# Rotary embedding of the second attention: order, number and memory of the VectorE instructions between the two attentions

## The chip, the cores and the metric

The kernel runs on one core of one Trainium2 chip. The metric is the device time of one execution in microseconds (us); the median of three runs is taken. TensorE does the matrix products, ScalarE (ACT in the profile) activations and copies, VectorE (DVE) and GpSimd (POOL) elementwise work; SyncE (SP) issues DMAs. PSUM is the memory into which TensorE writes, SBUF the large on-chip memory. GpSimd works on SBUF alone here.

## The reference

Two transformer layers over 2048 tokens of width 128, all in float32. Layer 0: a layer norm, an attention of 16 heads of 8 with an arccos kernel instead of softmax, and a gated feed-forward part, both added to the input. Layer 1, cut to what matters:

```
xn  = layernorm(x);  xa = layernorm(xn) * gamma + beta
q, k, v = split(xa @ w_qkv)                 # 16 heads of 64, each of q, k, v: 2048 x 1024
rotate(t): t1, t2 = halves of a head (32 + 32)
           [t1*cos - t2*sin, t2*cos + t1*sin]
scores = rotate(q) rotate(k)^T / 8;  out = softmax(scores) v;  x + out @ w_out + b_out + ffn(xn)
```

The change concerns `rotate` for q and k: 2048 tokens by 2048 values (q and k together).

## The kernel before

The program is a sequence of blocks: `stage_project0`, `stage_attention0`, `stage_project1`, `stage_attention1`, `stage_output`. Between blocks all engines meet. The change is in `stage_project1`, the stage between the attentions. It adds the output of attention 0 to the residual, does two layer norms and then a loop over 16 tiles (`k`) of 128 tokens each. The times and rows below speak mostly of this loop.

For each tile TensorE makes six banks of 512 float32 columns (`qkv(k, b)`, L1084, two matmuls per bank): b = 0 to 3 are q and k and go to the four banks of `psR`, b = 4 and 5 are v and go to the two banks of `psA`. A unit u = 4k + b is one bank of `psR`, which is 8 heads of q or k. A unit passes through these steps, each on its own engine, tied by semaphores:

1. VectorE rotates: cosine product from PSUM to `ra` (L965), two sine products of half the size from PSUM to `rb` (L967, L969), and the sum `ra + rb` into `ra` (L973). `ra` and `rb` have two buffers each (u % 2).
2. ScalarE rounds `ra` to float16 into `hl` (`high_qk`, L1004).
3. GpSimd computes the rest `ra - hl` into `hl` (L1048, semaphore `lo_ready`).
4. TensorE transposes the eight heads into `psB` (`turn_halves`, L1093).
5. ScalarE copies `psB` to `stg` (`stage`, L1023), and after every fourth tile (at the end after every second) SyncE stores `stg` to HBM.

For v, ScalarE writes a rounded half (`high_v`, L1013) and VectorE the rest (L979), two instructions per tile behind the four units. TensorE may overwrite bank b of `psR` with the next tile when the semaphore `rope_read` says so: before, that is at the end of the second sine product. `ra` is written again when `lo_ready` of unit u - 2 has come. The order of work on each engine is the order in which it is written in the code; there is no planner. On TensorE this order is: qkv(k+1,0), qkv(k+1,1), turn_halves(k,0), qkv(k+1,2), turn_halves(k,1), qkv(k+1,3), turn_halves(k,2), qkv(k+1,4), qkv(k+1,5), turn_halves(k,3). On ScalarE, per tile: high_qk 0, stage 3 of the tile before, high_v 0, high_qk 1, high_v 1, high_qk 2, stage 0, high_qk 3, stage 1, stage 2.

Of the kernel before, what the change touches and what calls it, by code (L numbers as in the profile page):

```python
# [6 lines left out]
ALU = mybir.AluOpType  # L7
# [7 lines left out]
P = 128  # L15
S = 2048
D = 128
NT = S // P
# [827 lines left out]
def stage_project1(nc, io, sb):  # L846
# [3 lines left out]
    HB = 8  # L850
    HALF = HD1 // 2
    with ExitStack() as ctx:
        def t(name, shape, dt=F32):
            return ctx.enter_context(nc.sbuf_tensor(name, shape, dt))

        def sem(name):
            return ctx.enter_context(nc.semaphore(name))
# [8 lines left out]
        cos_t, sin_t = t("cos_t", [P, NT, HALF]), t("sin_t", [P, NT, 2, HALF])  # L866
        ident_h = t("ident_h", [P, P], F16)
        ra, rb = t("ra", [P, 2, BANK]), t("rb", [P, 2, BANK])
# [4 lines left out]
        psR = ctx.enter_context(nc.psum_tensor("psR1", [P, 4, BANK], F32))  # L873
# [7 lines left out]
        xn_ready, xa_ready = sem("xn_ready1"), sem("xa_ready1")  # L881
        qkv_ps, rope_read = sem("qkv_ps1"), sem("rope_read")
        v_high, v_low = sem("v_high"), sem("v_low")
        rot_ready, hi_ready, lo_ready = sem("rot_ready"), sem("hi_ready"), sem("lo_ready")
        hl_ps, hl_taken = sem("hl_ps"), sem("hl_taken")

        v_stored = [sem("v_stored_0"), sem("v_stored_1")]
# [3 lines left out]
        with nc.Block() as block:  # L891
# [32 lines left out]
            @block.vector  # L924
            def _(eng):
                n = [0]

                def link(ins):
                    n[0] += 1
                    ins.then_inc(dve, 1)  # L930
                    eng.wait_ge(dve, n[0])

                eng.wait_ge(weights_loaded, 16 * 6)
                eng.tensor_copy(ident_h[:, :], ident[:, :])
                eng.memset(v_st[:, :, :, :, HD1:HD1 + 1], QS)
                eng.memset(v_st[:, :, :, :, VN:VW], 0.0)
                link(eng.tensor_tensor(base[:, :, :], base[:, :, :],
                                       b_out[:, :].unsqueeze(1).to_broadcast([P, NT, D]), ALU.add))
                for k in range(NT):
                    eng.wait_ge(out_ps, k + 1)  # L940
                    eng.tensor_tensor(base[:, k, :], base[:, k, :], psR[:, k % 4, 0:D], ALU.add).then_inc(x1_ready, 1)
                eng.wait_ge(x1_ready, NT)
                norm_on_vector(eng, link, base, xn, stats, mv, var, sd, tmp, var_ready, sd_ready, 1)
                eng.sem_inc(xn_ready, 1)
                norm_on_vector(eng, link, xn, xa, stats, mv, var, sd, tmp, var_ready, sd_ready, 2)
                link(eng.tensor_tensor(xa[:, :, :], xa[:, :, :], gamma[:, :].unsqueeze(1).to_broadcast([P, NT, D]),
                                       ALU.mult))
                eng.tensor_tensor(xa[:, :, :], xa[:, :, :], beta[:, :].unsqueeze(1).to_broadcast([P, NT, D]),
                                  ALU.add).then_inc(xa_ready, 1)

                eng.tensor_tensor(base[:, :, :], base[:, :, :], b_out1[:, :].unsqueeze(1).to_broadcast([P, NT, D]),
                                  ALU.add)

                eng.wait_ge(loaded, 32)
                for k in range(NT):
                    for b in range(4):
                        u = 4 * k + b

                        src = psR[:, b, :].rearrange("p (h a f) -> p h a f", h=HB, a=2)
                        a_ = ra[:, u % 2, :].rearrange("p (h a f) -> p h a f", h=HB, a=2)  # L960
                        b_ = rb[:, u % 2, :].rearrange("p (h a f) -> p h a f", h=HB, a=2)
                        eng.wait_ge(qkv_ps, 6 * k + b + 1)
                        if u >= 2:
                            eng.wait_ge(lo_ready, u - 1)
                        eng.tensor_tensor(a_, src, cos_t[:, k, :].unsqueeze(1).unsqueeze(1)  # L965
                                          .to_broadcast([P, HB, 2, HALF]), ALU.mult)
                        eng.tensor_tensor(b_[:, :, 0, :], src[:, :, 1, :],  # L967
                                          sin_t[:, k, 0, :].unsqueeze(1).to_broadcast([P, HB, HALF]), ALU.mult)
                        eng.tensor_tensor(b_[:, :, 1, :], src[:, :, 0, :],  # L969
                                          sin_t[:, k, 1, :].unsqueeze(1).to_broadcast([P, HB, HALF]), ALU.mult)\  # L970
                           .then_inc(rope_read, 1)
                        eng.wait_ge(rope_read, u + 1)
                        eng.tensor_tensor(ra[:, u % 2, :], ra[:, u % 2, :], rb[:, u % 2, :], ALU.add)\  # L973
                           .then_inc(rot_ready, 1)
                    for b in range(2):

                        eng.wait_ge(v_high, 2 * k + b + 1)
                        vv = v_st[:, k // 4 % 2, b * HB:(b + 1) * HB, k % 4, :]
                        eng.scalar_tensor_tensor(out=vv[:, :, HD1 + 1:VN],  # L979
                                                 in0=psA[:, b, :].rearrange("p (h e) -> p h e", h=HB), scalar=QS,  # L980
                                                 in1=vv[:, :, 0:HD1], op0=ALU.mult, op1=ALU.subtract)\
                           .then_inc(v_low, 1)

            @block.scalar
            def _(eng):
                for g in range(NCH):
                    eng.wait_ge(turned, g + 1)
                    eng.activation(attn0T[:, g * BANK:(g + 1) * BANK], psA[:, g % 2, :], ACT.Copy).then_inc(taken, 1)
                for i in range(2):
                    eng.wait_ge(var_ready, i + 1)  # L990
                    eng.activation(sd[:, :], var[:, :], ACT.Sqrt).then_inc(sd_ready, 1)
                    for g in range(NCH):
                        eng.wait_ge(turned, NCH * (i + 1) + g + 1)
                        dst = (xn2T, xaT)[i]
                        eng.activation(dst[:, g * BANK:(g + 1) * BANK], psA[:, g % 2, :], ACT.Copy).then_inc(taken, 1)

                def high_qk(k, b):

                    u = 4 * k + b
                    eng.wait_ge(rot_ready, u + 1)  # L1000
                    if k >= 2:

                        eng.wait_ge(hl_ps, 4 * (k - 1))
                    eng.activation(hl[:, k % 2, b * HB:(b + 1) * HB, 0, :],  # L1004
                                   ra[:, u % 2, :].rearrange("p (h e) -> p h e", h=HB), ACT.Copy)\
                       .then_inc(hi_ready, 1)

                def high_v(k, b):
                    eng.wait_ge(qkv_ps, 6 * k + 5 + b)
                    if k == 8 or k == 12:  # L1010

                        eng.wait_ge(v_stored[k // 4 % 2], 16)
                    eng.activation(v_st[:, k // 4 % 2, b * HB:(b + 1) * HB, k % 4, 0:HD1],  # L1013
                                   psA[:, b, :].rearrange("p (h e) -> p h e", h=HB), ACT.Copy, scale=QS)\
                       .then_inc(v_high, 1)

                def stage(k, g):

                    eng.wait_ge(hl_ps, 4 * k + g + 1)
                    if k % 4 == 0 and k >= 8:  # L1020

                        eng.wait_ge(qk_stored[k // 4 % 2], 32 * (k // 8))
                    eng.activation(stg[:, k // 4 % 2, g * HB:(g + 1) * HB, k % 4 * P:(k % 4 + 1) * P],  # L1023
                                   psB[:, g % 2, :].rearrange("p (h t) -> p h t", h=HB), ACT.Copy)\
                       .then_inc(hl_taken, 1)

                for k in range(NT):
                    high_qk(k, 0)
                    if k >= 1:
                        stage(k - 1, 3)  # L1030
                    high_v(k, 0)
                    high_qk(k, 1)
                    high_v(k, 1)
                    high_qk(k, 2)
                    stage(k, 0)
                    high_qk(k, 3)
                    stage(k, 1)
                    stage(k, 2)
                stage(NT - 1, 3)
# [620 lines left out]
```

## Time and profile before

| | |
|---|---|
| median of 3 runs | 3676.81 us (3673.8 to 3677.45) |
| the profiled execution: time, span | 3673.4 us, 3671.6 us |
| granted TensorE clock, mean over the span | 0.831 |
| loop over the 16 tiles, first VectorE instruction to last ScalarE instruction | 1996.40 to 2167.58 us |
| share of the span: PE, DVE, ACT, POOL | 85%, 77%, 82%, 73% |

A time in the profile is in microseconds from the start of the span. "DVE L973 ... 1.15" is the duration of one instruction; a bracket at the end of a line tells how long the engine stood idle before it and what it waited for. An instruction can start a little before the end that is shown for the one in front of it on its engine, so the spacing of two starts can be less than a duration.

### The profile page before, as it was taken

The page shows a single profiled execution, that of the slowest core. Times are in us where ns is not written, and L with a number is a line of the kernel's source. Part 1 is how long each engine was busy: PE and PEld are TensorE (multiplying, and loading weights), DVE is VectorE, ACT ScalarE, POOL GpSimd, SP SyncE. Part 2 cuts the span into 40 slices and gives each one's busy share as a digit, 9 for nine tenths or more (in the row PEclk, how much of TensorE's full clock was granted, in tenths as well). Part 3 has the DMA queues.
Part 4 walks back from the last instruction along what each step waited for, and adds up shares of the span by engine and source line. Part 5 has one row for each costly group of instructions (what it writes and reads, how often), then busy time and mean ns, then how long its engine had stood idle before and what let it go on. Part 6 is the DMA issues. An engine that isn't in the chain of part 4 may idle for free. (4 is left out here: it accounts for less than half of the span.)

```text
span 3671.6 us, 59781 instructions
## 1 busy us (share of the span) xinstructions
PE 3125.7 (85%) x19264; PEld 1305.2 (36%) x19264; DVE 2831.9 (77%) x4045; ACT 3014.8 (82%) x2658; POOL 2666.5 (73%) x1450
## 2 busy tenths in 40 slices
PE   4888888898888988889886758888888888888899
PEld 2322222222122221222213323555555555555547
DVE  7678988888888888888887977877878778788301
ACT  1799999999999999999995645887878888788822
POOL 2698988989889898898882424776767777677600
PEclk8776677766777667776677977999999999999999
DMA  0100000000000000000001450010000110000100
GB/s 23 53 7 7 1 6 7 6 7 2 4 7 6 7 4 3 7 6 6 5 5 38 139 161 24 25 47 25 24 25 24 34 38 24 25 24 25 39 0 12
DMA packets 59508, 85.46 MB, mean 23 GB/s; under 512 B 9808, under 2 KB 45904, under 8 KB 58960
## 3 DMA queue, kind: packets, MB, share of 16 engines
q1 hardware_dynamic: 59344, 83.06, 7.9%
q8 instruction: 129, 2.11, 0.2%
q14 instruction: 35, 0.29, 0.0%
HBM read 52.44 MB, written 30.54 MB: 23 GB/s over the span
## 5 line engine op out<-in xcount | busy, mean ns | idle before, releaser
L1177 POOL TENSOR_TENSOR lo<-pr,hi 128x1024 f16<-128x1024 f32 x384 | 917.3, 2412 | 383.8 <-ACT hi L1303 381.7
L1226 DVE TENSOR_REDUCE mx<-mx_ps 128x1 f32<-128x512 f32 x1024 | 660.0, 684 | 164.8 <-PE mx_ps L1341 161.5
L1318 ACT ACTIVATE pr<-s_ps 128x1024 f32<-128x1024 f32 x512 | 531.8, 1039 | 264.3 <-PE s_ps L1362 234.7
L1303 ACT ACTIVATE hi<-pr 128x1024 f16<-128x1024 f32 x512 | 548.1, 1071 | 0.0
L1341 PE MATMUL mx_ps<-ka,qa 128*128 128x512 f16 x1024 | 386.1, 398 | 142.4 <-DVE mx L1226 117.3
L671 ACT ACTIVATE wt<-wt 128x2048 f32<-128x2048 f32 x256 | 485.0, 1895 | 0.5
L477 POOL TENSOR_TENSOR wt<-base,wt 128x1024 f32<-128x1024 f32 x192 | 459.9, 2395 | 15.1
L662 ACT ACTIVATE wt<-wt,theta_bias 128x10240 f32<-128x10240 f32 (+2 forms) x96 | 464.3, 4837 | 0.8
L1381 PE MATMUL pv_ps<-vh,hi 128*128 128x129 f16 x4096 | 432.0, 222 | 11.6 <-ACT sums L1309 5.3
L1360 PE MATMUL s_ps<-qa,ka 128*128 128x512 f16 x1024 | 395.9, 387 | 35.2 <-issue 22.4
L473 POOL TENSOR_TENSOR base<-base,shift 128x1024 f32<-128x1024 f32 x192 | 363.7, 1894 | 84.6 <-DVE base L527 84.6
L1381 PE MATMUL pv_ps<-vh,lo 128*128 128x65 f16 x4096 | 417.9, 194 | 0.0
L1362 PE MATMUL s_ps<-qb,kb 65*128 65x512 f16 x1024 | 396.6, 387 | 0.0
L1381 PEld LDWEIGHTS pv_ps<-vh,hi 128*128 128x128 f16 x4096 | 372.1, 98 | 61.8 <-POOL lo L1177 11.5
L477 POOL TENSOR_TENSOR wt<-vb,wt 128x1024 f32<-128x1024 f32 x160 | 379.0, 2369 | 12.6
L1381 PEld LDWEIGHTS pv_ps<-vh,lo 128*128 128x128 f16 x4096 | 365.9, 98 | 55.9 <-issue 3.0
L750 PE MATMUL m_ps<-mst 110*128 110x512 f16 (+1 forms) x640 | 321.2, 609 | 47.5 <-ACT wt L651 19.7
L643 ACT ACTIVATE wt<-m_ps 128x1024 f32<-128x1024 f32 x352 | 333.1, 1033 | 25.8 <-PE m_ps L719 24.2
L473 POOL TENSOR_TENSOR vb<-vb,shift 128x1024 f32<-128x1024 f32 x160 | 302.9, 1893 | 60.3 <-DVE vb L527 60.3
L750 PE MATMUL r_ps<-mst 111*128 111x512 f16 (+1 forms) x768 | 315.0, 446 | 35.2 <-DVE wt L515 10.3
L1177 DVE TENSOR_TENSOR lo<-pr,hi 128x1024 f16<-128x1024 f32 x128 | 261.8, 2046 | 86.6 <-ACT hi L1303 86.6
L719 PE MATMUL m_ps<-mst 109*128 109x512 f16 x1024 | 308.3, 385 | 22.0 <-ACT wt L643 11.2
(197 smaller groups left out, 5292.7 us busy)
## 6 DMA issues: line engine op xcount, KB each, us to landing
qk<-stg SPq DMA_DIRECT2D x6, 2048.0 KB, 13.4
vh<-v SPq DMA_DIRECT2D x16, 520.0 KB, 3.5
qa<-qk SPq DMA_DIRECT2D x16, 512.0 KB, 3.3
ka<-qk SPq DMA_DIRECT2D x32, 256.0 KB, 4.8
v<-v_st SPq DMA_DIRECT2D x3, 2080.0 KB, 7.9
qst<-parts_dram SPq DMA_DIRECT2D x144, 32.0 KB
kst<-parts_dram SPq DMA_DIRECT2D x144, 32.0 KB
qk<-stg SPq DMA_DIRECT2D x4, 1024.0 KB, 8.7
```

Source lines behind the costliest of these rows:

```text
L473: eng.tensor_tensor(v, v, shift[:, 0:1].to_broadcast([P, 2 * BANK]), ALU.subtract)\
L477: eng.tensor_tensor(u, v, u, ALU.mult).then_inc(cubic, 1)
L662: eng.activation(wt[:, k:k + many, :], wt[:, k:k + many, :], ACT.Ln, bias=theta_bias[:, 0:1], scale=-2.0 if k >= NQ else -KA / (G4 * G4 * ...
L671: eng.activation(wt[:, k, :], wt[:, k, :], ACT.Exp, scale=GEXP, accum_out=n_c[:, k:k + 1])\
L750: mm = eng.matmul(slot(r)[:, cols(i, BANK)], mst[0:rows, 1, cols(k)], mst[0:rows, 0, rhs], start=True, stop=True)
L1177: eng.tensor_tensor(lo[:, i % NHL, :, :], pr_slot(i), hi[:, i % NHL, :, :], ALU.subtract).then_inc(lo_done, 1)
L1226: eng.tensor_reduce(mx4[:, q // NCH, q % NCH:q % NCH + 1], mx_ps[:, q % 2, :], AX.X, ALU.max)\
L1303: eng.activation(hi[:, i % NHL, :, :], pr_slot(i), ACT.Copy).then_inc(hi_done, 1)
L1318: eng.activation(pr_slot(i), s_ps[:, i % 2, :, :], ACT.Exp, scale=SM).then_inc(exp_done, 1)
L1360: eng.matmul(s_ps[:, i % 2, n_, :], ka[:, par, k * P:(k + 1) * P], qa[:, par, w], start=True, stop=False)
L1362: mm = eng.matmul(s_ps[:, i % 2, n_, :], kb[0:HD1 + 1, par, k * P:(k + 1) * P], qb[0:HD1 + 1, par, w], start=False, stop=True)
L1381: mm = eng.matmul(pv_ps[:, j // 2, j % 2 * OW:j % 2 * OW + cols], half[:, i % NHL, n_, j * P:(j + 1) * P], vh[:, par, k, 0:cols], start=(k ...
```

## The change

The sine product becomes one instruction of 512 elements per partition, which reads the bank with the halves of each head exchanged and writes `rb`. It comes first. The cosine product reads the same bank of `psR` and writes its result over it, in place. The sum then reads `psR` (PSUM) and `rb` (SBUF) and writes `ra`. `rope_read`, which allows TensorE to overwrite the bank, now comes with the sum, and ScalarE waits for the same semaphore in place of `rot_ready`. The instructions of neighbouring units are interleaved: sine(u), sum(u-1), cosine(u). For the last unit of all tiles but the last one, the sum comes after the two v instructions and the first sine product of the next tile.

```diff
+                def halves(ap):
+                    return ap.rearrange("p (h a f) -> p h a f", h=HB, a=2)
+                def sine(u):
+                    k, b = u // 4, u % 4
+                    eng.wait_ge(qkv_ps, 6 * k + b + 1)
+                    if u >= 2:
+                        eng.wait_ge(rope_read, u - 1)
+                    eng.tensor_tensor(halves(rb[:, u % 2, :]), halves(psR[:, b, :])[:, :, ::-1, :],
+                                      sin_t[:, k, :, :].unsqueeze(1).to_broadcast([P, HB, 2, HALF]),
+                                      ALU.mult).then_inc(sin_ready, 1)
+                def cosine(u):
+                    k, b = u // 4, u % 4
+                    eng.wait_ge(sin_ready, u + 1)
+                    eng.tensor_tensor(halves(psR[:, b, :]), halves(psR[:, b, :]),
+                                      cos_t[:, k, :].unsqueeze(1).unsqueeze(1).to_broadcast([P, HB, 2, HALF]),
+                                      ALU.mult).then_inc(cos_ready, 1)
+                def rotated(u):
+                    eng.wait_ge(cos_ready, u + 1)
+                    if u >= 2:
+                        eng.wait_ge(lo_ready, u - 1)
+                    eng.tensor_tensor(ra[:, u % 2, :], psR[:, u % 4, :], rb[:, u % 2, :], ALU.add)\
+                       .then_inc(rope_read, 1)
                 for k in range(NT):
-                    for b in range(4):
-                        u = 4 * k + b
-                        src = psR[:, b, :].rearrange("p (h a f) -> p h a f", h=HB, a=2)
-                        a_ = ra[:, u % 2, :].rearrange("p (h a f) -> p h a f", h=HB, a=2)
-                        b_ = rb[:, u % 2, :].rearrange("p (h a f) -> p h a f", h=HB, a=2)
-                        eng.wait_ge(qkv_ps, 6 * k + b + 1)
-                        if u >= 2:
-                            eng.wait_ge(lo_ready, u - 1)
-                        eng.tensor_tensor(a_, src, cos_t[:, k, :].unsqueeze(1).unsqueeze(1)
-                                          .to_broadcast([P, HB, 2, HALF]), ALU.mult)
-                        eng.tensor_tensor(b_[:, :, 0, :], src[:, :, 1, :],
-                                          sin_t[:, k, 0, :].unsqueeze(1).to_broadcast([P, HB, HALF]), ALU.mult)
-                        eng.tensor_tensor(b_[:, :, 1, :], src[:, :, 0, :],
-                                          sin_t[:, k, 1, :].unsqueeze(1).to_broadcast([P, HB, HALF]), ALU.mult)\
-                           .then_inc(rope_read, 1)
-                        eng.wait_ge(rope_read, u + 1)
-                        eng.tensor_tensor(ra[:, u % 2, :], ra[:, u % 2, :], rb[:, u % 2, :], ALU.add)\
-                           .then_inc(rot_ready, 1)
+                    for u in range(4 * k, 4 * k + 4):
+                        sine(u)
+                        if u >= 1:
+                            rotated(u - 1)
+                        cosine(u)
+                    if k == NT - 1:
+                        rotated(4 * NT - 1)
...
                 def high_qk(k, b):
-                    eng.wait_ge(rot_ready, u + 1)
+                    eng.wait_ge(rope_read, u + 1)
```

## Rows read from the trace of the kernel before

**Rows 1.** The profile's page: the span, and VectorE's busy time over it.

```profile
span 3671.6 us, 59781 instructions
...
PE 3125.7 (85%) x19264; PEld 1305.2 (36%) x19264; DVE 2831.9 (77%) x4045; ACT 3014.8 (82%) x2658; POOL 2666.5 (73%) x1450
```

**Rows 2.** Busy time by stretch: the loop; granted clock (PEclk), DMA share behind it.

```profile
1995.00:2164.00 169.00, 128.53 (x696) 63.49 (x696) 165.39 (x287) 111.57 (x158) 72.74 (x63) 0.98 0.42 132
```

**Rows 3.** Waits in the loop, 1996 to 2180: total us, times, longest.

```profile
ACT hl L1004 <- DVE ra L973: 56.8, 64, 3.4
...
DVE ra L965 <- PE psR L1084: 3.6, 1, 3.6
```

**Rows 4.** Groups of instructions, VectorE, same stretch: busy us, mean ns.

```profile
L973 DVE TENSOR_TENSOR ra<-ra,rb 128x512 f32<-128x512 f32 x64 | 66.1, 1033 | 2.2
L965 DVE TENSOR_TENSOR ra<-psR,cos_t 128x512 f32<-128x512 f32 x64 | 43.4, 679 | 3.6 <-PE psR L1084 3.6
```

**Rows 5.** Timeline of VectorE over one tile: start us, duration us.

```profile
2058.32 1.28 DVE L979 SCALAR_TENSOR_TENSOR v_st<-psA,v_st 128x512 f16<-128x512 f32 x2
2059.52 0.68 DVE L965 TENSOR_TENSOR ra<-psR,cos_t 128x512 f32<-128x512 f32 x1
2060.12 0.41 DVE L967 TENSOR_TENSOR rb<-psR,sin_t 128x256 f32<-128x256 f32 x1
2060.45 0.41 DVE L969 TENSOR_TENSOR rb<-psR,sin_t 128x256 f32<-128x256 f32 x1
2060.89 0.69 DVE L973 TENSOR_TENSOR ra<-ra,rb 128x512 f32<-128x512 f32 x1
2061.50 0.68 DVE L965 TENSOR_TENSOR ra<-psR,cos_t 128x512 f32<-128x512 f32 x1
...
2062.43 0.41 DVE L969 TENSOR_TENSOR rb<-psR,sin_t 128x256 f32<-128x256 f32 x1
2062.88 1.15 DVE L973 TENSOR_TENSOR ra<-ra,rb 128x512 f32<-128x512 f32 x1
2063.95 0.68 DVE L965 TENSOR_TENSOR ra<-psR,cos_t 128x512 f32<-128x512 f32 x1
...
2068.84 1.28 DVE L979 SCALAR_TENSOR_TENSOR v_st<-psA,v_st 128x512 f16<-128x512 f32 x2
```

**Rows 6.** Timeline of GpSimd over the same tile.

```profile
2059.14 1.16 POOL L1048 TENSOR_TENSOR hl<-ra,hl 128x512 f16<-128x512 f32 x1 [1.29 <-ACT hl L1004]
2062.33 1.15 POOL L1048 TENSOR_TENSOR hl<-ra,hl 128x512 f16<-128x512 f32 x1 [2.03 <-ACT hl L1004]
```

**Rows 7.** The first VectorE instruction, the last sum and the last ScalarE copy.

```profile
1996.40 0.69 DVE L965 TENSOR_TENSOR ra<-psR,cos_t 128x512 f32<-128x512 f32 x1 [3.55 <-PE psR L1084]
...
2162.39 1.15 DVE L973 TENSOR_TENSOR ra<-ra,rb 128x512 f32<-128x512 f32 x1
...
2166.56 1.02 ACT L1023 ACTIVATE stg<-psB 128x1024 f16<-128x1024 f16 x1 [0.53 <-PE psB L1093]
```

**Rows 8.** Tile t_ps in attention 0: duration ns, minimum/median/maximum.

```profile
L582 DVE TENSOR_TENSOR t_ps<-t_ps,small x16: 184/185/190, 329.4 to 1955.7; 128x16 f32<-128x16 f32 x16
...
L588 DVE TENSOR_TENSOR small<-small,t_ps x16: 181/183/185, 330.1 to 1956.5; 128x16 f32<-128x16 f32 x16
```

**Rows 9.** Groups of instructions, ScalarE, in the loop.

```profile
L1023 ACT ACTIVATE stg<-psB 128x1024 f16<-128x1024 f16 x64 | 62.9, 1008 | 0.5 <-PE psB L1093 0.5
L1004 ACT ACTIVATE hl<-ra 128x512 f16<-128x512 f32 x64 | 40.3, 630 | 56.8 <-DVE ra L973 56.8
L1013 ACT ACTIVATE v_st<-psA 128x512 f16<-128x512 f32 x32 | 18.7, 584 | 0.6 <-PE psA L1084 0.6
```

**Rows 10.** Timeline of TensorE where it runs without waits, early in the loop.

```profile
2000.42 1.88 PE L1084 MATMUL psR<-w_qkv,attn0T 128*128 128x512 f32 x4
...
2002.14 0.61 PE L1093 MATMUL psB<-ident_h,hl 128*128 128x128 f16 x8
...
2002.58 1.08 PE L1084 MATMUL psR<-w_qkv,attn0T 128*128 128x512 f32 x2
```

More of the change, by code:

```diff
@@ L883, in stage_project1 @@
         v_high, v_low = sem("v_high"), sem("v_low")
-        rot_ready, hi_ready, lo_ready = sem("rot_ready"), sem("hi_ready"), sem("lo_ready")
+        sin_ready, cos_ready = sem("sin_ready"), sem("cos_ready")
+        hi_ready, lo_ready = sem("hi_ready"), sem("lo_ready")
         hl_ps, hl_taken = sem("hl_ps"), sem("hl_taken")
```

## The prediction

> **What bounds the kernel now.** I read the page first: no engine is busy all the time (DVE 77% of a span of 3671.6 us, [rows 1]), so the answer lies in the stage of the change. Its loop over 16 tiles, between about 1995 and 2168 us, is a different picture: in a stretch of 169.0 us VectorE is busy 165.4 us, TensorE 128.5, ScalarE 111.6, GpSimd 72.7, at a granted clock of 0.98 [rows 2]. The waits say the same from the other side. ScalarE waits 64 times, 56.8 us in all, for VectorE's sum, while VectorE has waited once, 3.6 us, before the first unit [rows 3]. VectorE bounds the loop, all of its instructions are in series, and what shortens them shortens the kernel: the engines meet behind the stage, and nothing of the next stage starts earlier by itself.
>
> The timeline of one tile shows what the time goes to [rows 5]. From the pair of v instructions at 2058.32 to the next pair at 2068.84 it is 10.52 us; 16 times 10.52 is 168.3, which is the loop. Spacing of starts: a product of 512 elements 0.60 (2059.52 to 2060.12), a sine half 0.33, the second half 0.44, because the sum behind it waits for its end (0.41 + 0.03), the sum 0.61 or 1.07. The sums are of two kinds, 0.69 and 1.15 us. The mean of 64 is 1033 ns [rows 4], which is 48 of 1.15 and 16 of 0.69: three of four are long. The long one at 2062.88 starts while GpSimd runs from 2062.33 to 2063.48, the short one at 2060.89 behind the end of a GpSimd run (2059.14 + 1.16 = 2060.30) [rows 5, 6]. So a sum of two SBUF operands is stretched by 0.46 us when GpSimd works beside it.
>
> Products with one operand in PSUM are not: the cosine product at 2059.52 lies wholly under the GpSimd run that ends at 2060.30 and takes 0.68, and the sine half at 2062.43 lies wholly under the next and takes 0.41, as those outside do [rows 5, 6].
>
> **The change, part by part.** It has four effects on VectorE, per tile:
>
> 1. The sum reads PSUM and SBUF, as the cosine product did. By the rows it should then cost that product's 0.68 us, spacing 0.60, GpSimd or not. Three sums fall from 1.07 to 0.60 and one from 0.61 to 0.60: 1.42 us.
> 2. Two sine halves become one instruction: 0.33 + 0.33 becomes 0.60, four times 0.06: 0.24 us. The exchanged halves are runs of 32 elements, which each half read before at no cost that shows: 0.409 against 0.679 us for 256 against 512 elements is 1.05 ns per element and a fixed part. Were the single instruction as dear as the halves, 0.24 us is lost again.
> 3. The wait of the sum for the instruction right in front of it goes: sine(u), sum(u-1), cosine(u) each wait for something at least two places back. Four times 0.11: 0.44 us.
> 4. The cosine product writes PSUM, the bank that it reads. This form at this size is not in the trace. The nearest rows are 16 elements wide: 185 ns in place in PSUM, 183 ns to SBUF [rows 8]. The 2 ns are 0.13 ns per element, or 0.06 us at 512 elements, 4 us in 64 units. A bank that served a read or a write by turns would double 1.05 ns per element; 16 elements would then show 17 ns, not 2. I take 0, with 4 us as the mild upper end; no row speaks for a gain.
>
> The new tile is 12 instructions at 0.60 and two v instructions at 0.60 (2058.32 to 2059.52 is 1.20 for two): 8.40 us. 10.52 - 8.40 = 2.12, and the parts give 1.42 + 0.24 + 0.44 = 2.10.
>
> From the first VectorE instruction to the end of the last sum it is now 2163.54 - 1996.40 = 167.1 us [rows 7]. In the new order 64 + 64 + 63 products and sums and 30 v instructions precede the last sum: 221 x 0.60 + 0.11 (it does wait for the cosine in front of it) + 0.68 = 133.4. The edge takes 1.0 back, see below: 134.4. The tail (rounding, rest, transposes, copy: 4.0 us to 2167.58) and the stores behind it stay. That is 32.7 us less. A second semaphore on an instruction may cost 0.01 (0.61 behind a sum, 0.60 behind a cosine [rows 5]); sine and sum both carry two, 127 x 0.01 = 1.3. I take 32.
>
> Two rules of the Trainium skill speak for less. "VectorE: DVE Perf Modes", section on the TRN2 errata, gives a PSUM source a fixed part of 120 cycles and an SBUF source 58; at 0.96 GHz that is 0.065 us more per sum, 4.1 us in all. The rows have 0.679 us for the product out of PSUM and 0.69 for the unstretched sum out of SBUF [rows 4, 5], no such step. The same page, section "The DRAIN you can't avoid", says that a semaphore between Vector instructions costs nothing; by it part 3 would be worth nothing, 7.0 us less. The rows have 0.33 us of spacing without and 0.44 with the wait behind the same shape [rows 5]. By both rules the gain would be about 21 us.
>
> **Can the others keep a pace of 8.40?** ScalarE has 4 x 1.008 + 4 x 0.630 + 2 x 0.584 = 7.72 us per tile [rows 9], less in spacing. TensorE, where it runs free, needs 1.72 us for two banks and 0.44 for eight transposes [rows 10]: 6 x 0.86 + 4 x 0.44 = 6.9. GpSimd 4 x 1.15 = 4.6. All fit, ScalarE with least room.
>
> Two loops get tighter. The bank of `psR` is freed at the sum: about 3.1 us after the start of its sine instead of 1.4 after the start of its cosine. The same bank's next sine starts at least 7.2 us after the last one, so 4 us are left for two matmuls of 1.1; TensorE has, in its queue, transposes ahead of them, but no wait longer than that chain. The two buffers of `ra` are tighter: sum(u) needs the rest of u-2. From the start of a sum: 0.68 + 0.03 + 0.63 (rounding) + 0.08 + 1.15 (rest) + 0.03 = 2.60 us, against 3.60 for two units. That leaves 1.0 for whatever ScalarE is doing, and a copy is 1.01. Laying out the orders of all engines by these spacings I get 0.4 us of slack in the middle of the loop, and one wait, about 1.0 us, of the very last sum for the rest of unit 61, since no v pair lies between them. That is the 1.0 above. Behind the delayed fourth sum of a tile (v pair and a sine come first, 1.8 us) are queued ScalarE's rounding and two copies and TensorE's qkv(k+1,3); VectorE asks for that bank only four units later.
>
> SyncE stores after every fourth tile, and the DMA share is 0.42 in the stretch [rows 2]; with 34 in place of 42 us between stores it becomes some 0.5. The clock is 0.98 and TensorE gets denser, so no reason for a fall.
>
> **The rivals.**
> - In place costs a second pass (cosine +0.54 us). Against it [rows 8], which are small. Tile 8.40 + 2.16 = 10.56, nothing gained: 3677. Chance 0.05.
> - The sum out of PSUM is stretched by GpSimd all the same, all four per unit at 1.07: 4 x (0.60 + 0.60 + 1.07) + 1.20 = 10.28, a gain of 0.24 x 16 = 4: 3673. Against it [rows 5, 6]. Chance 0.04.
> - The new waits cost as the old one: 12 x 0.71 + 1.20 = 9.72, a gain of 0.80 x 16 = 13: 3664. For it: there are more semaphores. Against: they are set an instruction earlier. Chance 0.06.
> - The buffers of `ra` bind: if ScalarE does a v half and a copy (0.58 + 1.01) ahead of each rounding, two units need 4.2 us; 4 x 2.1 + 1.20 = 9.6, a gain of 15: 3662. For it: the slack is only 0.4. Chance 0.05.
> - Slower: in place costs far more than a second pass. It decides from 2.12 / 4 = 0.53 us per cosine; at two more passes (+1.08) the tile is 12.72, 2.2 x 16 = 35 us more: 3712. Same evidence against it. Chance 0.04.
> - My forecast: 0.76.
>
> **The numbers.** The sum is against the profiled execution: 3673.4 - 32 = 3641.4. The median of the runs shown is 3.4 above that execution, so 3644.8. Bounds of the likeliest: a spacing of 0.54 (1.05 ns x 512, no fixed part at all) would save 11 more, but ScalarE's 7.72 stops it near -40; sine as dear as the halves +4, in place +4, both rules +11. Its own range, and the one that holds 8 in 10, is 3637 to 3656; all rivals lie above. About 0.2%, 7.4 us, is what a measurement can tell. Faster 0.76 + 0.06 + 0.05 = 0.87, same 0.05 + 0.04 = 0.09, slower 0.04.
>
> **What the profile after would show.** Right: sums of 0.68 in all 64 units, one sine form of 128x512 at 0.68, cosine to `psR` at 0.68 to 0.74, v pairs 8.4 to 8.5 us apart, VectorE still without waits, ScalarE's wait for the sum down from 56.8 to about 15 us. Wrong: a sum that stays at 1.15 beside GpSimd, a cosine above 0.8, spacings of 0.71 with durations of 0.68, or VectorE waiting for GpSimd's rest in every tile.

## The result and the profile after

The changed kernel took 3644.13 us, median of 4 runs (3643.80 to 3645.42), against 3675.31 (4 runs, 3672.14 to 3677.45) of the kernel before. The ratio is 0.9917, 95% interval 0.9899 to 0.9934: some 30.5 us less. Forecast were 3644.8 us and a range of 3637 to 3656.

The profiled execution took 3644.35 us. First the groups of instructions on VectorE in the stretch 1960 to 2180 (busy us, mean ns), which answer to [rows 4]:

```profile
L972 DVE TENSOR_TENSOR psR<-psR,cos_t 128x512 f32<-128x512 f32 x64 | 44.1, 690 | 0.0
L964 DVE TENSOR_TENSOR rb<-psR,sin_t 128x512 f32<-128x512 f32 x64 | 43.4, 678 | 4.7 <-PE psR L1102 4.7
L981 DVE TENSOR_TENSOR ra<-psR,rb 128x512 f32<-128x512 f32 x64 | 43.4, 677 | 1.3 <-POOL hl L1066 1.3
```

The sum fell from a mean of 1033 ns to 677. The single sine is as dear as a cosine of its size. The cosine in place takes 12 ns more than the 678 of the other products. VectorE's timeline over one tile, which answers to [rows 5]:

```profile
2080.22 1.28 DVE L997 SCALAR_TENSOR_TENSOR v_st<-psA,v_st 128x512 f16<-128x512 f32 x2
2081.41 0.68 DVE L964 TENSOR_TENSOR rb<-psR,sin_t 128x512 f32<-128x512 f32 x1
2082.01 0.68 DVE L981 TENSOR_TENSOR ra<-psR,rb 128x512 f32<-128x512 f32 x1
2082.61 0.69 DVE L972 TENSOR_TENSOR psR<-psR,cos_t 128x512 f32<-128x512 f32 x1
2083.21 0.68 DVE L964 TENSOR_TENSOR rb<-psR,sin_t 128x512 f32<-128x512 f32 x1
2083.80 0.68 DVE L981 TENSOR_TENSOR ra<-psR,rb 128x512 f32<-128x512 f32 x1
...
2088.59 1.28 DVE L997 SCALAR_TENSOR_TENSOR v_st<-psA,v_st 128x512 f16<-128x512 f32 x2
```

GpSimd in the same tile, for [rows 6]:

```profile
2083.43 1.16 POOL L1066 TENSOR_TENSOR hl<-ra,hl 128x512 f16<-128x512 f32 x1 [0.85 <-ACT hl L1022]
```

Every start is 0.60 us behind the one before (a row with x2 holds two instructions). The sum at 2083.80 lies wholly under GpSimd's run of 2083.43 to 2084.59 and takes 0.68 all the same; 47 of the 64 sums overlap a run of GpSimd, and all 64 take 0.68 or 0.69. From one v pair to the next it is 8.37 us, against 10.52 before. The waits of the stretch, for [rows 3]:

```profile
ACT hl L1022 <- DVE ra L981: 14.7, 17, 5.2
...
DVE rb L964 <- PE psR L1102: 4.7, 2, 4.5
DVE ra L981 <- POOL hl L1066: 1.3, 1, 1.3
```

ScalarE's 64 waits for the sum, 56.8 us, have become 17 of 14.7 us. VectorE waits for GpSimd once, before the very last sum; its only other waits are for the first two banks from TensorE (4.5 and 0.2 us). First and last instructions of the loop, for [rows 7], from the timelines of VectorE and ScalarE:

```profile
1997.86 0.69 DVE L964 TENSOR_TENSOR rb<-psR,sin_t 128x512 f32<-128x512 f32 x1 [4.50 <-PE psR L1102]
...
2131.79 0.69 DVE L981 TENSOR_TENSOR ra<-psR,rb 128x512 f32<-128x512 f32 x1 [1.26 <-POOL hl L1066]
```

```profile
2135.51 1.02 ACT L1041 ACTIVATE stg<-psB 128x1024 f16<-128x1024 f16 x1 [0.53 <-PE psB L1111]
```

The loop is 2136.53 - 1997.86 = 138.7 us, before 171.2: 32.5 us less. The span is only 29.0 us less (3642.6 against 3671.6). The loop began 1.5 us later, and from its end to the end of the span it was 1506.1 us against 1504.0. Neither can be put down to the change: in two more profiled executions of the same changed kernel (a1 and a2 below) the loop began at 1996.39 and 1995.68 us, and that last part was 1500.9 and 1512.9 us, while the loop was 138.4 in both. The loop repeats to 0.3 us and the rest of the kernel does not repeat to 10. So the experiments are read by the loop and the tile, and by whole times only where the difference is large.

### The profile page after: what moved, and what is told of

It is laid out like the page before. It is cut to its first block and busy times, and to the rows that moved or that the text cites. A ratio compares the mean times of both kernels' runs of the same rounds, so it can differ in the third digit from the quotient of the medians.

```text
span 3642.6 us, 59779 instructions
## 1 busy us (share of the span) xinstructions
PE 3123.6 (86%) x19264; PEld 1306.7 (36%) x19264; DVE 2800.0 (77%) x3981; ACT 3013.6 (83%) x2658; POOL 2666.2 (73%) x1450
## 5 line engine op out<-in xcount | busy, mean ns | idle before, releaser
L750 PE MATMUL r_ps<-mst 111*128 111x512 f16 (+1 forms) x768 | 314.5, 445 | 35.0 <-DVE wt L515 10.2
```

What stands on the lines that cost most here:

```text
L750: mm = eng.matmul(slot(r)[:, cols(i, BANK)], mst[0:rows, 1, cols(k)], mst[0:rows, 0, rhs], start=True, stop=True)
```

## The experiments

The question is not whether the stage got faster but which of the parts did it, and whether the mechanism is the one named: a VectorE instruction with two SBUF operands held by GpSimd. Tile and loop below are from the profiled execution of each; e1 to e5 are single executions.

| kernel | tile, us | loop, us | time, us |
|---|---|---|---|
| before | 10.52 | 171.2 | 3676.81 (median, 3 runs) |
| e3: one sine, nothing else | 10.45 | 170.0 | 3675.8 |
| e2: one sine, new order, sum from SBUF | 10.68 | 173.4 | 3674.3 |
| e1: one sine, sum from PSUM, in series | 9.42 | 153.7 | 3659.5 |
| e4: kernel before, GpSimd only writes, once | 9.15 | 149.1 | 3653.4 |
| e5: kernel before, GpSimd only writes, twice | 9.15 | 149.2 | 3649.3 |
| changed kernel | 8.37 | 138.7 | 3644.13 (median, 4 runs) |

The single runs e1 to e4 had one run of the kernel before beside them, 3682.13 us; e5 had nine, with a median of 3676.33.

**e1, the units in series.**

```diff
                     for u in range(4 * k, 4 * k + 4):
                         sine(u)
-                        if u >= 1:
-                            rotated(u - 1)
                         cosine(u)
-                    if k == NT - 1:
-                        rotated(4 * NT - 1)
+                        rotated(u)
```

> The changed kernel, but the three instructions of a unit stand in series (sine, cosine, sum of the same unit), so that the cosine waits for the sine right in front of it and the sum for the cosine. My theory (a wait for the instruction in front costs 0.11 us of spacing): per unit 0.71 + 0.71 + 0.60 = 2.02 us, a tile of 4 x 2.02 + 1.20 = 9.28 us instead of 8.37, 14 us more than the changed kernel, about 3658. Rival (such a wait costs nothing, as a rule of the Trainium skill has it): tile still 8.4, about 3644.

Timeline of VectorE in e1:

```profile
2045.28 0.68 DVE L964 TENSOR_TENSOR rb<-psR,sin_t 128x512 f32<-128x512 f32 x1
2045.99 0.70 DVE L972 TENSOR_TENSOR psR<-psR,cos_t 128x512 f32<-128x512 f32 x1
2046.72 0.69 DVE L981 TENSOR_TENSOR ra<-psR,rb 128x512 f32<-128x512 f32 x1
2047.33 0.68 DVE L964 TENSOR_TENSOR rb<-psR,sin_t 128x512 f32<-128x512 f32 x1
```

The spacing is 0.71 from sine to cosine, 0.73 from cosine to sum, 0.61 from sum to the next sine. A wait for the instruction right in front costs 0.11 to 0.13 us, and the tile is 9.42 (2042.02 to 2051.44), close to the 9.28 expected and far from 8.4. The new order is worth 1.05 us a tile against this series, which has two such waits in a unit; the kernel before has one. The rival rule, that such a semaphore is free, does not hold here.

**e2, the new order with a sum of two SBUF operands.**

```diff
-                    eng.tensor_tensor(halves(psR[:, b, :]), halves(psR[:, b, :]),
+                    if u >= 2:
+                        eng.wait_ge(lo_ready, u - 1)
+                    eng.tensor_tensor(halves(ra[:, u % 2, :]), halves(psR[:, b, :]),
...
-                    if u >= 2:
-                        eng.wait_ge(lo_ready, u - 1)
-                    eng.tensor_tensor(ra[:, u % 2, :], psR[:, u % 4, :], rb[:, u % 2, :], ALU.add)\
+                    eng.tensor_tensor(ra[:, u % 2, :], ra[:, u % 2, :], rb[:, u % 2, :], ALU.add)\
```

> The changed kernel in order and number of instructions, but the cosine product goes to ra in SBUF, as before, and the sum reads ra and rb, both in SBUF. My theory (a sum with two SBUF operands is stretched beside GpSimd, and this was two thirds of the gain): most sums take up to 1.15 us again, mean above 0.95, tile 10.0 to 10.6 us, 3670 to 3679 in all, nearly nothing left of the gain. Rival (the gain came from order and merging; the stretch goes when the sum starts elsewhere in GpSimd's run): sums at 0.69, tile 8.4, about 3644.

Timelines of VectorE (its sums) and of GpSimd in e2:

```profile
2048.33 0.67 DVE L981 TENSOR_TENSOR ra<-ra,rb 128x512 f32<-128x512 f32 x1
...
2050.13 1.32 DVE L981 TENSOR_TENSOR ra<-ra,rb 128x512 f32<-128x512 f32 x1
...
2052.57 1.42 DVE L981 TENSOR_TENSOR ra<-ra,rb 128x512 f32<-128x512 f32 x1
...
2055.11 1.58 DVE L981 TENSOR_TENSOR ra<-ra,rb 128x512 f32<-128x512 f32 x1
```

```profile
2049.74 1.16 POOL L1066 TENSOR_TENSOR hl<-ra,hl 128x512 f16<-128x512 f32 x1 [1.84 <-ACT hl L1022]
2052.29 1.16 POOL L1066 TENSOR_TENSOR hl<-ra,hl 128x512 f16<-128x512 f32 x1 [1.38 <-ACT hl L1022]
2054.99 1.15 POOL L1066 TENSOR_TENSOR hl<-ra,hl 128x512 f16<-128x512 f32 x1 [1.55 <-ACT hl L1022]
```

The sums last 1.32, 1.42 and 1.58 us, yet each ends 0.55, 0.54 and 0.55 us behind the end of GpSimd's run (2050.90, 2053.45, 2056.14). The same holds for all 143 long sums of the kernel before, e2 and e3: each ends 0.53 to 0.56 us behind GpSimd. A sum slowed by a factor would get more of its work done the more of GpSimd's run it meets (here 0.77, 0.88 and 1.03 us), and would have less left behind GpSimd's end. So the sum is not slowed by a factor: it stands still until GpSimd is done or nearly done, and the earlier in GpSimd's run it starts, the longer it looks. Tile 10.68 (2046.54 to 2057.22), 0.16 more than before the change: order and merging alone lose, and the rival is out. The mechanism came as expected, its size did not: the sums were to take up to 1.15 us and the tile 10.0 to 10.6.

**e3, one sine instruction in the kernel before.**

```diff
-                        eng.tensor_tensor(b_[:, :, 0, :], src[:, :, 1, :],
-                                          sin_t[:, k, 0, :].unsqueeze(1).to_broadcast([P, HB, HALF]), ALU.mult)
-                        eng.tensor_tensor(b_[:, :, 1, :], src[:, :, 0, :],
-                                          sin_t[:, k, 1, :].unsqueeze(1).to_broadcast([P, HB, HALF]), ALU.mult)\
+                        eng.tensor_tensor(b_, src[:, :, ::-1, :],
+                                          sin_t[:, k, :, :].unsqueeze(1).to_broadcast([P, HB, 2, HALF]), ALU.mult)\
                            .then_inc(rope_read, 1)
```

> The kernel before with one edit: the two sine halves are one instruction with exchanged halves. My theory: it takes 0.68 us, spacing 0.60 plus 0.11 for the wait of the sum, in place of 0.33 + 0.44: tile 10.52 - 4 x 0.06 = 10.28, 4 us less than before. Since the sum then starts 0.06 earlier in GpSimd's run and ends where GpSimd lets it, the gain can vanish in the three stretched sums: between 1 and 4 us. Rival (exchanged halves in one instruction are as dear as two halves or dearer): duration above 0.74, no gain.

VectorE and GpSimd in e3:

```profile
2050.11 0.68 DVE L967 TENSOR_TENSOR rb<-psR,sin_t 128x512 f32<-128x512 f32 x1
2050.82 1.21 DVE L971 TENSOR_TENSOR ra<-ra,rb 128x512 f32<-128x512 f32 x1
```

```profile
2050.33 1.15 POOL L1046 TENSOR_TENSOR hl<-ra,hl 128x512 f16<-128x512 f32 x1 [1.97 <-ACT hl L1002]
```

The sine takes 0.68 as expected, but the sum grew from 1.15 to 1.21: it starts 0.06 us earlier in GpSimd's run and still ends 0.55 us behind its end (2051.48, 2052.03). Only the one unstretched unit of a tile gains: tile 10.45 (2046.39 to 2056.84), 0.07 less, loop 170.0 against 171.2, at the low end of the 1 to 4 us expected.

**e4 and e5, GpSimd only writes.** Both are the kernel before with the rests of q and k left out.

```diff
-                    eng.tensor_tensor(dst[:, :, 1, :], ra[:, u % 2, :].rearrange("p (h e) -> p h e", h=HB),
-                                      dst[:, :, 0, :], ALU.subtract).then_inc(lo_ready, 1)
+                    eng.memset(scratch[:, u % 4, :], 0.0)        # e5 only
+                    eng.memset(dst[:, :, 1, :], 0.0).then_inc(lo_ready, 1)
```

> The kernel before, but GpSimd writes zeros in place of the rest of q and k (the low halves are left out, so the scores lack them), an instruction that reads nothing. My theory (the stretch of the sum comes from both engines reading SBUF): all 64 sums at 0.69 us, tile 4 x (0.60 + 0.33 + 0.44 + 0.61) + 1.20 = 9.12 us, 22 us less than before. Rival (any GpSimd work on SBUF stretches a VectorE instruction that works on SBUF alone): sums that overlap it stay well above 0.69.

> As the run in which GpSimd only writes zeros in place of the rest of q and k (the low halves are left out), but each time it first writes zeros to a scratch tile too, so that its run of writes lasts over 1 us and the sum starts inside it; in the run with one write each write was over 0.05 us before the sum began, so that run could not tell. My theory (the stretch needs reads of SBUF by GpSimd): all sums 0.69 us, tile 9.1 to 9.2. Rival (any GpSimd instruction on SBUF holds the sum): most sums above 1.0 us.

In e4 all sums took 0.69 us (mean 692 ns), the tile 9.15 and the loop 149.1, as forecast; but each write was over just before the sum began, so the run says nothing on what kind of GpSimd work holds a sum. It does say what the hold costs the kernel before: 10.52 - 9.15 = 1.37 us a tile. In e5 the writes reach into it. GpSimd and VectorE in e5:

```profile
2053.89 0.53 POOL L1049 MEMSET scratch<- 128x512 f32 x1 [2.19 <-ACT hl L1005]
...
2054.36 0.53 POOL L1050 MEMSET hl<- 128x512 f16 x1
...
2054.47 0.69 DVE L974 TENSOR_TENSOR ra<-ra,rb 128x512 f32<-128x512 f32 x1
```

The sum starts at 2054.47 inside the write of 2054.36 to 2054.89, in SBUF both, and takes 0.69; held as in e2 it would have ended at 2055.44 and taken 0.97. The same is so of 48 of the 64 sums, and their mean is 692 ns. A GpSimd write of zeros does not hold the sum. GpSimd's subtraction and its write of zeros differ in kind and in length too, so that it is the reading which holds the sum is argued, not shown alone. The loop is 149.2.

**a1, e6, e7, then a2, e8, e9: is there more?** Two edits of the changed kernel, each timed in four or five executions beside five of a copy of it. e6 puts the v instructions of the last tile ahead of the last sum; e7 moves one of the two v rests of a tile to GpSimd:

```diff
+                def copy_v(k):                                    # ScalarE, behind high_v(k, 1)
+                    if k >= 2:
+                        eng.wait_ge(v_lowg, k - 1)
+                    eng.activation(vf[:, k % 2, :], psA[:, 1, :], ACT.Copy, scale=QS).then_inc(v_copied, 1)
...
+                    if b == 3:                                    # GpSimd, behind the fourth rest of a tile
+                        vv = v_st[:, k // 4 % 2, HB:2 * HB, k % 4, :]
+                        eng.wait_ge(v_copied, k + 1)
+                        eng.tensor_tensor(vv[:, :, HD1 + 1:VN], vf[:, k % 2, :].rearrange("p (h e) -> p h e", h=HB),
+                                          vv[:, :, 0:HD1], ALU.subtract).then_inc(v_lowg, 1)
```

> The changed kernel again, on the same chip as the two below and in five rounds, to measure their small steps against: 30 to 33 us under the kernel before.

> The changed kernel, but in the last tile the two v instructions come before the last sum. They fill the 1.26 us in which VectorE waits there for GpSimd's rest of unit 61. My theory (that wait is bound by GpSimd and the last sum then starts when it did): end of the loop unchanged within 0.2 us, the v store issued 1.9 us earlier, and at best 1 to 2 us less in the stores behind the loop; within noise in all. Rival (the v pair delays the last sum): loop 0.5 to 1 us longer.

> The changed kernel with one of the two v rests of a tile moved from VectorE to GpSimd: ScalarE makes a float32 copy of that bank of psA in SBUF (0.5 us of spacing more on ScalarE), GpSimd subtracts from it (1.15 us more on GpSimd). If VectorE still bounds the loop by itself: tile 8.37 - 0.60 = 7.77, 16 x 0.60 = 9.6 us less than the changed kernel. Rival (ScalarE, whose work comes to about 6.9 us of spacing in the tile and now 7.4, and the two buffers of ra bind at this pace): VectorE waits for GpSimd's rests in each tile, tile 8.0 to 8.4, gain 0 to 5 us.

| run | loop, us | median, us | lowest to highest |
|---|---|---|---|
| a1, the changed kernel | 138.4 | 3644.24 | 3637.41 to 3646.35 |
| e6 | 138.4 | 3644.74 | 3640.02 to 3647.84 |
| e7 | 132.3 | 3640.02 | 3637.46 to 3644.01 |
| a2, the changed kernel | 138.4 | 3648.66 | 3642.72 to 3649.55 |
| e8, as e7 | 132.0 | 3639.88 | 3638.95 to 3642.46 |
| e9, e7 and e6 together | 132.0 | 3637.42 | 3635.50 to 3643.12 |

e6: nothing. In its profile the time between the last ScalarE copy and the table load that opens the next stage is 9.3 us, 0.9 less than in a1; that is lost in the spread.

e7: the tile is 7.94 us (2052.02 to 2059.96), between the two cases. Timelines of VectorE, GpSimd and ScalarE in e7:

```profile
2052.02 0.68 DVE L1001 SCALAR_TENSOR_TENSOR v_st<-psA,v_st 128x512 f16<-128x512 f32 x1
2052.61 0.68 DVE L968 TENSOR_TENSOR rb<-psR,sin_t 128x512 f32<-128x512 f32 x1
2053.37 0.69 DVE L985 TENSOR_TENSOR ra<-psR,rb 128x512 f32<-128x512 f32 x1
2053.98 0.69 DVE L976 TENSOR_TENSOR psR<-psR,cos_t 128x512 f32<-128x512 f32 x1
```

```profile
2052.11 1.16 POOL L1076 TENSOR_TENSOR hl<-ra,hl 128x512 f16<-128x512 f32 x1 [1.51 <-ACT hl L1026]
```

```profile
2050.92 0.59 ACT L1035 ACTIVATE v_st<-psA 128x512 f16<-128x512 f32 x1
2051.40 0.63 ACT L1026 ACTIVATE hl<-ra 128x512 f16<-128x512 f32 x1
...
2057.95 1.02 ACT L1050 ACTIVATE stg<-psB 128x1024 f16<-128x1024 f16 x1 [0.65 <-PE psB L1126]
```

VectorE still starts an instruction every 0.60 us, but for one sum in each tile, which starts 0.76 behind the sine in front of it: the sum at 2053.37 needs GpSimd's rest that ends at 2053.27. With that one wait of 0.16 us the tile comes to 13 x 0.60 + 0.16 = 7.96. The rest is late because ScalarE's rounding in front of it (2051.40) stands in the queue behind a copy and a v half. ScalarE itself pauses 0.65 us in a tile, for TensorE's transposes. So the buffers of `ra` bind, as in the second case of the forecast, and the pace comes from a chain through all four engines; no run shows one of them as the one that sets it. The loop is 6.0 us shorter than in a1 (138.36 - 132.33 = 6.0), and 1.8 us come back behind it: from the last copy to the table load of the next stage it is 12.0 us in place of 10.2. Why is not shown.

> The changed kernel once more, as the base for the two below: about 3644, 30 to 33 us under the kernel before.

> The kernel with one v rest of each tile on GpSimd, again, because its times and those of the changed kernel overlapped. Its loop was 6.3 us shorter than that of the changed kernel (tile 7.94 us, ScalarE then without idle time but for 0.64 us a tile), and 1.8 us of it came back in the wait for the stores. My theory: 4 to 5 us less than the changed kernel. Rival: no difference that can be measured.

> The same with the v instruction of the last tile ahead of the last sum. If the last sum and the stores gain from it, up to 1 us less than the run above; otherwise the same, within noise in either case.

The medians of e7 and e8 lie 4.2 and 8.8 us under the copy of the changed kernel beside them, the loops 6.0 and 6.4. All four times of e8 lie below the five of a2, those of e7 and a1 overlap, and so do the intervals of the ratios to the kernel before: 0.9923 (0.9909 to 0.9937) for a2, 0.9908 (0.9893 to 0.9923) for e8, 0.9901 (0.9886 to 0.9917) for e9. So moving the rest likely makes the whole kernel faster too, by some 4 to 9 us. That the loop is shorter is shown; the size of the gain over the whole kernel is not. e9 against e8 shows nothing: the loops are equal, and the times overlap.

a1 and a2 also time the change itself twice more: 32.1 and 25.6 us less than the kernel before by the medians, 0.9913 and 0.9923 by the ratio. The 30 to 33 us expected were met by a1 and missed by a2, whose loop is the same 138.4.

## Why the prediction was right

The bound was read rightly: VectorE in series, and the loop moved with its spacing. The tile was forecast at 8.40 us and is 8.37; the loop at 134.4 + 4.0 = 138.4 and is 138.7 and twice 138.4. The last sum was to wait about 1.0 us for the rest of unit 61; it waits 1.26. ScalarE's wait for the sum was to fall to about 15 us; it is 14.7, but the prediction shows no working for the 15. The second semaphore on an instruction, priced at 0.01 us, costs nothing that shows: the spacing is 0.60 throughout. The DMA share in the loop was to rise from 0.42 to some 0.5 and is 0.54, and the granted clock is 0.99 after 0.98 (from 1998 to 2130 us; VectorE is busy 131.76 us of 132):

```profile
1998.00:2130.00 132.00, 118.71 (x678) 60.64 (x676) 131.76 (x221) 107.03 (x153) 70.14 (x61) 0.99 0.54 169
```

The buffers of `ra` did not bind in any other unit, but by less than the 0.4 us of slack that the prediction gives. The tightest place in a tile is the sum of its third unit, which needs GpSimd's rest of the first:

```profile
2085.97 1.16 POOL L1066 TENSOR_TENSOR hl<-ra,hl 128x512 f16<-128x512 f32 x1 [1.38 <-ACT hl L1022]
```

```profile
2087.39 0.68 DVE L981 TENSOR_TENSOR ra<-psR,rb 128x512 f32<-128x512 f32 x1
```

From the end of the rest (2087.13) to the start of the sum are 0.26 us, and where a sum does wait for a rest, in e7, this step takes 0.10 (2053.27 to 2053.37). So 0.16 us are left, and the rival in which these buffers bind was nearer than the prediction had it. e7, with one more ScalarE instruction in a tile, runs into it.

The sum: forecast 32 us less, measured 32.5 in the loop and 29.0 in the span, 30.5 by the ratio. The difference is the rest of the kernel, which varies by more than that. So that the loop came out as forecast speaks for the working; that the median, 3644.13, lies 0.7 us from the forecast 3644.8 is luck, as the 3648.66 of a2 shows. One bound was worked out wrongly, without effect on the forecast: ScalarE's 7.72 us in a tile would stop the gain near 44 us ((10.52 - 7.72) x 16 = 44.8), not near 40.

In place: taken at 0, bounded at +0.06 us per cosine. The duration is 690 ns, against 678 in e2 for the cosine in the same order that writes SBUF, and the spacing is unchanged. The inference from 16 elements, that there is no second pass, held.

The split into parts holds only in the order in which the prediction takes them, the hold first. It priced the stretch of a sum at 0.46 us as if fixed, and the sine, the sum and the wait as if they added. e2 and e3 show that a held sum ends 0.55 us behind GpSimd's run wherever it starts. So while the hold stands, what makes VectorE reach a held sum earlier is given back at that sum. The merge, priced at 0.24 us a tile, is worth 0.07 by itself (e3), and the new order on top of it minus 0.23 (10.45 to 10.68). Taking the hold away alone, priced at 1.42, is worth 1.37 (e4); what is then left, 9.15 to 8.37, is 0.78 against 0.68 priced for merge and order. The sum from PSUM is worth 1.03 in series (10.45 to 9.42), where the cosine in place also has to wait for the sine, about 0.5 us a tile by the spacings of e1 and e3 (4 x 0.13), and 2.31 in the new order (10.68 to 8.37). So the sum from PSUM is worth about half of the gain by itself, and it is what lets the other two parts count. The prices came to the right total because it was made together with them.

The first of the two rules of the Trainium skill that spoke for less falls with the rows after: the sum out of PSUM takes 677 ns, the one out of SBUF without company 692 (e5), not 65 more. Both with a wait for the instruction in front of them, it is 691 (e1) and 692 (e5). The second falls with e1, at least for these products and sums; the page measured a row of copies, which no run here repeats. What holds the sum is told by another page of the Trainium skill, "SBUF — State Buffer", section "Who interferes with whom": a VectorE instruction with two SBUF inputs contends with a GpSimd instruction that reads SBUF, not with one that only writes, and one with at most one SBUF input does not contend. e2 (held), e5 (writes alone, not held) and the rows after (one input in PSUM, not held) agree with all three. It had a consequence that the prediction did not draw: the loser blocks until the other is done, and so the loss depends on where it starts.

## What to carry to other kernels

When an instruction of one form shows two durations, lay its start and end beside the other engines' runs: here the long ones all ended about 0.55 us behind GpSimd's end, which told a hold from a slowdown. While such a hold stands, savings ahead of it are given back; remove it first, for instance by leaving one operand in PSUM, and then fill the gap behind a dependent instruction with another unit's work. When whole times vary by some 10 us outside the stage, judge the edit by the stage's own length.

## What the runs showed of the hardware that was not expected

A held VectorE instruction of 0.69 us ends 0.55 us behind the shown end of the GpSimd instruction (e2: 1.32, 1.42 and 1.58 us of duration, all with that end). Either some 0.14 us of its work is done while it is held, or it is let go 0.14 us before GpSimd's end as the profile shows it; no run tells which. A product of 512 float32 columns written over the PSUM bank that it reads costs 690 ns against 678 for one that writes SBUF; whether the target or the shared bank costs the 12 ns is open. The halves of a head read from PSUM in exchanged order cost nothing: 678 ns for the sine (rows after), 679 for the cosine before [rows 4]. A wait for the VectorE instruction right in front costs 0.11 to 0.13 us of spacing (e1), one for an instruction two places back costs nothing that shows: 0.60 in the changed kernel, as from the cosine to the first sine half before, where nothing is waited for [rows 5].
